# Values that sequencers read, packed in words of 24 bits, in a graph kernel with four residual layers

## The chip, the cores and the metric

The kernel runs on one core of one Trainium2 chip. The metric is the device time of one execution in microseconds (us).

## What is computed

A graph has 3125 nodes with 64 features and 100000 edges, sorted by destination. Four blocks follow each other, each of them `x = x + layer(relu(layernorm(x)))`:

- block 0, three transformer convolutions: for each edge `alpha = q[dst] . (k[src] + e) / 8` with `e = edge_attr_64 @ We`; a softmax of alpha over the edges with the same destination; the sum over these edges of `softmax * (v[src] + e)`; plus `x @ Ws + bs`, relu, and a layer norm after the first two;
- block 1, ten steps of a propagation over the graph, `h = 0.9 * norm * sum(h[src] * norm[src]) + 0.1 * h0`;
- block 2, one graph convolution with degree norms and `edge_attr_32`;
- block 3, one attention layer with a softmax over the edges of a destination.

The three convolutions of block 0 go over the edges; blocks 1 and 3 work with a dense matrix of edge counts that is built on the way.

## The kernel before, in words

Destinations are cut in `NB` = 25 blocks of 128 nodes. Edges come in groups of 128; two groups are a batch (`BT` = 2). There are `NG` = 391 batches of edges, and `T` = `NBAT` = 415 batches of slots, as a batch that crosses into the next block of destinations is gone through once for each block. Which batch of edges, and which block, belongs to slot batch `j` depends on the data: the first phase computes it on VectorE (L456 to L476) and leaves it as rows of int32 on one partition each. SP copies them to where they stay (L306 to L308). The rows are: `ring_row`, the place in the ring of edge batches (0 to 54); `done_row`, how many edge batches must have landed; `brow`, the block (0 to 24); `free_row`, the last slot batch that needs an edge batch (SP frees its place behind it); `w4row`, the column offset in the matrix of edge counts for each of `T4` = 595 window slots; `flag_row`, 0 or 128 for each of these, which picks the zero half or the identity half of `identz`.

`row_values` (L91) emits one TENSOR_LOAD that puts n words of such a row into n registers of one engine's sequencer. In the trace all these loads stand under L93. With `REGS` = 5 the rows that go by `j` are read five words at a time; `w4row` and `flag_row` 17 at a time (`ADJ_ROW`), 3 or 10 at the start of a layer.

The body of `conv(l)` runs once for each layer. All engines work through a list that is written out in full, with semaphores between them.

- POOL (L217) gathers the node rows of each batch of edges with two indirect DMAs, into a ring of `RBAT` = 55 batches, after a wait on `free`.
- SP (L635 to L644) waits until the last user of a ring place is done (`bmm` against a value of `free_row`, L639, L640), gives it free, starts the load of the edge attributes (L642), and reports the batch of four before as landed (L631).
- ACT makes one-hot matrices of the destinations (L678, L681), sums products (L691), copies windows of edge counts out of PSUM (L699) and stores them to memory (`store_counts`, L704 to L710), at an offset from `w4row`.
- PE expands node values to edges (`expand`, L771, with `block_of`), aggregates edges to nodes (`aggregate`, L775 to L789, with `ring_row`), counts sources (L798), and adds window counts (`window_counts`, L812 and L814, with `flag_row`).
- DVE multiplies (`product`, L898 to L908, with `ring_row` and `done_row`), makes the one-hot operands (L916, L917, L924, L926), the weighted one-hots (`weighted`, L939, in layer 2 also L943 with `ring_row`), adds results to their block (`add`, L952, with `block_of`), and does the softmax of a window of up to 90 groups (L959 and on).

Slot batches are cut in windows of 45 batches (eight of them), 30, 15 and 10. While window w goes through expand and product, window w - 1 goes through weighted, aggregate and add. So one step of the loop has batch `j` of the first kind and batch `j` - 45 of the second. Between two windows stands the softmax of the window that was just gone through. Buffers between engines are two or three deep: expand of `j` waits for product `j` - 2, aggregate for add `j` - 2, product for the sums `j` - 3.

```python
if j % REGS == 0:
    regs[1] = row_values(nc, ET.DVE, ring_row, j, REGS, RBAT - 1)
    regs[2] = row_values(nc, ET.DVE, done_row, j, REGS, NG, 1)
dve.wait_ge(s["landed"], regs[2][j % REGS] & 1023)
```

Of the kernel before, what the change touches and what calls it, by code (L numbers as in the profile page):

```python
# [24 lines left out]
ADJ_ROW = 17  # L25
# [14 lines left out]
REGS = 5  # L40
# [87 lines left out]
def build(nc, a, out):  # L128
# [9 lines left out]
    with ctx:  # L138
# [46 lines left out]
        flag_row, done_row, free_row = [arena[32 * q:32 * q + 1, w4:w4 + T4].bitcast(i32) for q in (1, 2, 3)]  # L185
# [69 lines left out]
        with phase(nc, "qp ldd ldx ldw lds cst cio cnt gi ms p1 p2 p3 c1 c2 c3 mm mc st var std h row tr key ktr kc xs wr") as (block, s):  # L255
# [27 lines left out]
            CI, BI, RI, LI, FI, FQ = [V(tmp.take(n), n, dt=i32, parts=1) for n in (T, T, T, T, T4, NG)]  # L283
            SRT = V(tmp.take(NC), NC, dt=i32)
            MQ = V(tmp.take(L * AB), L, AB)
# [4 lines left out]
            def _(sp):  # L290
# [16 lines left out]
                for to, fr in ((ring_row, RI), (brow, BI), (flag_row, FI), (done_row[:, 0:T], LI), (free_row[:, 0:NG], FQ)):  # L307
                    sp.dma_start(to, fr).then_inc(s["wr"], 16)  # L308
# [5 lines left out]
                sp.wait_ge(s["wr"], 16 * 9)  # L314
# [89 lines left out]
            def _(dve):  # L404
                st = Steps(dve, s["st"])
                dve.wait_ge(s["ldd"], 32)
# [55 lines left out]
                st.link(dve.tensor_scalar(BI, WH[:, 0:T], float(NB - 1), None, ALU.min))  # L462
# [10 lines left out]
                st.link(dve.tensor_scalar(RI, CI, float(-(-65536 // RBAT)), None, ALU.mult))  # L473
                st.link(dve.tensor_single_scalar(RI, RI, 16, ALU.logical_shift_right))
                st.link(dve.scalar_tensor_tensor(RI, RI, float(-RBAT), CI, ALU.mult, ALU.add))
# [62 lines left out]
        def conv(l):  # L538
# [67 lines left out]
            with phase(nc, names) as (block, s):  # L606
# [19 lines left out]
                def _(sp):  # L626
# [6 lines left out]
                    last_slots = {}  # L633
# [21 lines left out]
                def _(act):  # L655
# [45 lines left out]
                    def store_counts(k):  # L701

                        t = adj0 + k
                        if k == 0 or t % ADJ_ROW == 0:  # L704
                            wins[0] = row_values(nc, ET.Activation, w4row, t, ADJ_ROW - t % ADJ_ROW, (NW4 - 1) * NB * WIN)
                            wins[1] = t
# [3 lines left out]
                        act.dma_start(adj_t[:, bass.ds(wins[0][t - wins[1]], NB * WIN)], ACC[t % 3]).then_inc(s["kst"], 16)  # L710
# [37 lines left out]
                def _(pe):  # L748
# [26 lines left out]
                    def aggregate(j):  # L775

                        if j % REGS == 0:
                            rings[0] = row_values(nc, ET.PE, ring_row, j, REGS, RBAT - 1)
# [3 lines left out]
                        r = rings[0][j % REGS]  # L782
# [942 lines left out]
```

## Time and profile before

| | us |
|---|---|
| median of 3 runs | 5708.73 |
| the runs | 5693.49, 5708.73, 5719.92 |
| the profiled execution | 5753.34 |
| its span, first to last instruction | 5751.5 |

| engine | busy, us | share of the span |
|---|---|---|
| PE | 3721.8 | 65% |
| DVE | 3245.0 | 56% |
| ACT | 2445.1 | 43% |
| POOL | 2353.9 | 41% |

The mean granted clock of TensorE is 0.76 of its full speed. Register, semaphore and DMA-issuing instructions are run by an engine's sequencer; they are not counted as busy, and the rows give their durations with a q behind the engine's name (DVEq). "Idle before" is the time that the engine stood still just before an instruction; "issue" as its releaser means that it waited for nothing that the profile can name, such as its own sequencer.

### The profile page before, as it was taken

To read this page: it belongs to the slowest core of one execution; us is meant where nothing else is said; L and a number is where in the kernel's file an instruction comes from. 1 tells how busy PE (TensorE), PEld (TensorE's weight loads), DVE (VectorE), ACT (ScalarE), POOL (GpSimd) and SP (SyncE) were. 2 spreads that over 40 slices of the span, in tenths; PEclk is the share of its full clock that TensorE was granted. 3 is DMA by queue.
4 is the path that set the end of the run, shared out by engine and by line. 5 is a ranking of instruction groups with operands and counts; after the bars stand their busy time and mean duration, and the time that the engine had idled before them with its cause. 6 is when DMAs were issued, how large, how long until landed. Compare 5 with 4: busy or idle time off the path is not lost. (4 is left out here: it accounts for less than half of the span.)

```text
span 5751.5 us, 96272 instructions
## 1 busy us (share of the span) xinstructions
PE 3721.8 (65%) x23392; PEld 3092.1 (54%) x23392; DVE 3245.0 (56%) x10295; ACT 2445.1 (43%) x8519; POOL 2353.9 (41%) x2436
## 2 busy tenths in 40 slices
PE   2466666665516666666664277777777749999566
PEld 1355544554414555444443166766666649999322
DVE  5366665565605665665554156656666643334699
ACT  0455555564306555655541265555553320000266
POOL 7255555555071555555532445555555020000000
PEclk9977687777756777777875577767776759999688
DMA  2233333333031333333321223333333040000000
GB/s 67 60 80 82 82 90 95 96 98 83 26 72 52 80 79 80 97 98 96 95 68 40 54 74 81 82 76 78 80 79 74 23 161 2 2 2 2 1 3 4
DMA packets 552348, 372.37 MB, mean 65 GB/s; under 512 B 399844, under 2 KB 476740, under 8 KB 551811
## 3 DMA queue, kind: packets, MB, share of 16 engines
q1 hardware_dynamic: 353891, 144.09, 9.8%
q10 hardware_dynamic: 121536, 142.57, 8.1%
q0 software_dynamic: 76384, 79.48, 7.3%
q8 instruction: 224, 3.67, 0.3%
q14 instruction: 313, 2.56, 0.1%
HBM read 300.59 MB, written 65.24 MB: 64 GB/s over the span
## 5 line engine op out<-in xcount | busy, mean ns | idle before, releaser
L217 POOL DMA_INDIRECT arena<-node_table,arena x1564 | 1513.6, 968 | 1262.6 <-SPq L640 831.8
L784 PE MATMUL ps<-arena 128*128 x4980 | 1078.6, 354 | 374.4 <-issue 150.4
L784 PEld LDWEIGHTS ps<-arena 128*128 128x128 f32 x4980 | 900.8, 254 | 496.0 <-issue 491.7
L908 DVE TENSOR_TENSOR arena<-ps,arena 128x258 f32<-128x258 f32 x1245 | 524.1, 421 | 1056.9 <-issue 706.7
L691 ACT ACTIVATE arena<-arena 128x129 f32<-128x129 f32 x2490 | 743.2, 301 | 794.7 <-DVE arena L908 403.9
L939 DVE TENSOR_SCALAR arena<-arena 128x128 f32<-128x128 uint16 x2490 | 877.9, 357 | 304.6 <-remote 110.8
L217 POOL DMA_INDIRECT arena<-last_node_table,arena x782 | 747.2, 955 | 640.3 <-SPq L640 415.5
L771 PE MATMUL ps<-arena 128*128 x2496 | 557.8, 362 | 193.6 <-issue 134.5
L771 PE MATMUL ps<-arena,e 128*128 x2484 | 551.7, 360 | 143.7 <-issue 69.8
L771 PEld LDWEIGHTS ps<-arena 128*128 128x128 f32 x2496 | 473.3, 257 | 272.6 <-issue 259.1
L1226 PE MATMUL ps<-arena 128*128 128x192 bf16 x6875 | 590.3, 247 | 18.4 <-issue 7.8
L1226 PEld LDWEIGHTS ps<-arena 128*128 128x128 bf16 x6875 | 586.6, 98 | 21.7 <-issue 13.8
L771 PEld LDWEIGHTS ps<-arena,e 128*128 128x128 f32 x2484 | 465.9, 255 | 219.4 <-issue 207.8
L812 PE MATMUL ps<-stage,al 128*128 128x400 bf16 x1190 | 398.2, 427 | 277.6 <-issue 172.1
L691 ACT ACTIVATION_READ_ACCUMULATOR arena<-arena 128x1 f32 x2490 | 468.0, 188 | 0.0
L952 DVE TENSOR_TENSOR arena<-arena,ps 128x129 f32 (+1 forms) x1245 | 363.5, 292 | 156.8 <-issue 59.3
L699 ACT ACTIVATE al<-ps 128x400 bf16<-128x400 f32 x397 | 197.3, 497 | 411.1 <-PE ps L814 113.9
L678 ACT ACTIVATE arena<-arena 128x256 f32<-128x256 bf16 x624 | 312.0, 500 | 93.3 <-issue 63.2
L678 ACT ACTIVATE e<-arena 128x256 f32<-128x256 bf16 x621 | 310.4, 500 | 89.9 <-issue 61.2
L926 DVE TENSOR_SCALAR stage<-arena 128x400 bf16<-128x400 uint16 x1190 | 345.0, 331 | 0.0
L789 PEld LDWEIGHTS ps<-arena 128*128 128x128 f32 x1660 | 309.4, 261 | 0.0
L789 PE MATMUL ps<-arena 128*128 x1660 | 293.7, 309 | 0.0
(340 smaller groups left out, 4209.4 us busy)
## 6 DMA issues: line engine op xcount, KB each, us to landing
arena<-in_attr SPq DMA_DIRECT2D x1173, 96.0 KB
arena<-slot_rows ACTq DMA_DIRECT2D x249, 320.0 KB
edge_counts<-al ACTq DMA_DIRECT2D x397, 100.0 KB
arena<-node_table,arena POOLq DMA_INDIRECT x1564
edge_counts<-stage ACTq DMA_DIRECT2D x198, 100.0 KB
arena<-last_node_table,arena POOLq DMA_INDIRECT x782
arena<-edge_counts SPq DMA_DIRECT2D x24, 500.0 KB, 5.4
stage<-edge_counts SPq DMA_DIRECT2D x16, 500.0 KB, 5.8
```

Source lines behind the costliest of these rows:

```text
L217: pool.indirect_dma_start(out=RING[:, t % R_SLOTS, XO:XO + n], out_offset=None, in_=table[:, :], in_offset=bass.IndirectOffsetOnAxis(ap=ID ...
L678: act.activation(o, ROWB[r % 2][:, (j % 5) * BT * P:(j % 5 + 1) * BT * P], ACT.Square, bias=pid1, scale=-1.0)\
L691: ins = act.activation(PR[j % 3][:, q], PR[j % 3][:, q], ACT.Copy, accum_out=AL[w % 2][:, c:c + 1])
L771: ins = pe.matmul(UPS[j % 2][:, q * AB:(q + 1) * AB], OHT[j % 6][:, q * P:(q + 1) * P], U[:, bass.ds(b, 1), :].rearrange("p a b -> p (a b) ...
L784: ins = pe.matmul(BPS[j % 2][:, 0:AB], WOH[j % 2][:, q], RINGS[:, bass.ds(r, 1), q, D32:D32 + AB].rearrange("p o f -> p (o f)"), start=q = ...
L789: ins = pe.matmul(BPS[j % 2][:, AB:CW], WOD[j % 2][:, q], RINGS[:, bass.ds(r, 1), q, 0:D32].rearrange("p o f -> p (o f)"), start=q == 0, s ...
L812: ins = pe.matmul(WPS, LOH[k % 3][:, q], KOH[k % 3][q], start=q == 0, stop=t == 0 and q == G4 - 1)
L908: dve.tensor_tensor(PR[j % 3], UPS[j % 2].rearrange("p (a b) -> p a b", b=AB), rows, ALU.mult)\
L926: ins = dve.tensor_scalar(KOH[k % 3][q], iota1[:, 0:NB * WIN], KEY4[:, adj0 + k, q:q + 1], None, ALU.is_equal)
L939: ins = dve.tensor_scalar(WOH[j % 2][:, q], iota1[:, 0:P], DZT[:, t:t + 1], PT[w % 2][:, c:c + 1], ALU.is_equal, ALU.mult)
L952: dve.tensor_tensor(to, to, BPS[j % 2], ALU.add).then_inc(s["add"], 1)
L1226: last = pe.matmul(ps[:, o + 256 * c:o + 256 * c + 3 * D], adj3[:, sx, bass.ds((d0 + c) * P, P)], g3[:, sx].rearrange("p a b -> p (a b)"), ...
```

## The change

The rows for sequencers are packed on VectorE in the first phase, several values in a word of at most 24 bits, and read a word at a time. `row_values` goes; `word_value` reads one word, `word_values` n words, and `field` takes a value out of a word by shift and mask.

- `REGS` is 4. `brow` has 4 blocks of 5 bits in a word. `ring_row` has two words for four batches: 4 ring places of 6 bits, and then the landed count of the first batch with the differences of the other three (2 bits each). `done_row` goes.
- `w4row` has 3 windows of 8 bits in a word (`ADJ_WIN` = 3), and the offset is multiplied out on ACT's sequencer. `flag_row` has 17 flags of one bit in a word.
- `free_row` is not packed; SP reads its words one at a time.

```diff
-def row_values(nc, eng, row, at, n, top, low=0):
+def word_value(nc, eng, row, at):
+
+    return word_values(nc, eng, row, at, 1)[0]
+
+
+def word_values(nc, eng, row, at, n):
 
     return nc.values_load_multi_w_load_instructions(
-        row[0:1, at:at + n], engines=[eng], min_val=low, max_val=top,
-        skip_runtime_bounds_check_because="the rows hold groups, blocks and windows of slots, which are in range for any edges")[1]
+        row[0:1, at:at + n], engines=[eng], min_val=0, max_val=(1 << 24) - 1,
+        skip_runtime_bounds_check_because="the words hold fields of 24 bits together")[1]
+
+
+def field(nc, word, at, bits, top):
+
+    v = (word >> at) & ((1 << bits) - 1) if at else word & ((1 << bits) - 1)
+    return nc.s_assert_within(v, 0, top, skip_runtime_bounds_check_because="the fields hold groups, blocks and windows of slots, in range for any edges")
...
+                def pack(to, values, per, bits):
+
+                    n = values.shape[1]
+                    full, words = n // per, -(-n // per)
+                    part = PK[:, 0:words]
+                    if words > full:
+                        st.link(dve.memset(part, 0.0))
+                    for k in range(per):
+                        v = values[:, k::per]
+                        if k:
+                            st.link(dve.scalar_tensor_tensor(part[:, 0:v.shape[1]], v, float(1 << bits * k), part[:, 0:v.shape[1]],
+                                                             ALU.mult, ALU.add))
+                        else:
+                            st.link(dve.tensor_copy(part[:, 0:v.shape[1]], v))
+                    st.link(dve.tensor_copy(to[:, 0:words], part))
...
-                st.link(dve.tensor_scalar(BI, WH[:, 0:T], float(NB - 1), None, ALU.min))
+                st.link(dve.tensor_scalar(WH[:, 0:T], WH[:, 0:T], float(NB - 1), None, ALU.min))
+                pack(BI, WH[:, 0:T], REGS, 5)
...
-                st.link(dve.tensor_scalar(w4row, WH[:, 0:T4], float(NB * WIN), None, ALU.mult))
+                pack(w4row, WH[:, 0:T4], ADJ_WIN, 8)
...
-                st.link(dve.tensor_scalar(FI, FR[:, 0:T4], float(P), None, ALU.mult))
+                pack(FI, FR[:, 0:T4], ADJ_ROW, 1)
...
-                dve.tensor_scalar(LI, CI, 1.0, None, ALU.add)
...
+                pack(RI[:, 0::2], WH[:, 0:T], REGS, 6)
+                st.link(dve.tensor_scalar(WH[:, 0:NREG], CI[:, 0::REGS], 1.0, None, ALU.add))
+                for k in range(1, REGS):
+                    n = CI[:, k::REGS].shape[1]
+                    st.link(dve.tensor_tensor(PK[:, 0:n], CI[:, k::REGS], CI[:, 0::REGS][:, 0:n], ALU.subtract))
+                    st.link(dve.scalar_tensor_tensor(WH[:, 0:n], PK[:, 0:n], float(1 << 7 + 2 * k), WH[:, 0:n], ALU.mult, ALU.add))
+                st.link(dve.tensor_copy(RI[:, 1:2 * NREG:2], WH[:, 0:NREG]))
...
-                            at = i - RBAT + 1
-                            if at % REGS == 1:
-                                last_slots[0] = row_values(nc, ET.SP, free_row, at, min(REGS, NG - RBAT + 1 - at), T, 1)
-                            sp.wait_ge(s["bmm"], last_slots[0][(at - 1) % REGS] & 1023)
+                            sp.wait_ge(s["bmm"], word_value(nc, ET.SP, free_row, i - RBAT + 1) & 1023)
...
-                        if k == 0 or t % ADJ_ROW == 0:
-                            wins[0] = row_values(nc, ET.Activation, w4row, t, ADJ_ROW - t % ADJ_ROW, (NW4 - 1) * NB * WIN)
-                            wins[1] = t
+                        if k == 0 or t % ADJ_WIN == 0:
+                            wins[0] = word_value(nc, ET.Activation, w4row, t // ADJ_WIN)
...
-                        act.dma_start(adj_t[:, bass.ds(wins[0][t - wins[1]], NB * WIN)], ACC[t % 3]).then_inc(s["kst"], 16)
+                        act.dma_start(adj_t[:, bass.ds(field(nc, wins[0], 8 * (t % ADJ_WIN), 8, NW4 - 1) * (NB * WIN), NB * WIN)], ACC[t % 3]).then_inc(s["kst"], 16)
...
                         if j % REGS == 0:
-                            rings[0] = row_values(nc, ET.PE, ring_row, j, REGS, RBAT - 1)
+                            rings[0] = word_value(nc, ET.PE, ring_row, j // REGS * 2)
...
-                        r = rings[0][j % REGS]
+                        r = field(nc, rings[0], 6 * (j % REGS), 6, RBAT - 1)
...
-                            flags[0] = row_values(nc, ET.PE, flag_row, t, ADJ_ROW - t % ADJ_ROW, P)
-                            flags[1] = t
+                            flags[0] = word_value(nc, ET.PE, flag_row, t // ADJ_ROW)
...
-                            ins = pe.matmul(WPS, identz[:, bass.ds(flags[0][t - flags[1]], P)], ACC[(t - 1) % 3], start=False, stop=True)
+                            ins = pe.matmul(WPS, identz[:, bass.ds(field(nc, flags[0], t % ADJ_ROW, 1, 1) * P, P)], ACC[(t - 1) % 3], start=False, stop=True)
...
                         if j % REGS == 0:
-                            regs[0] = row_values(nc, ET.PE, brow, j, REGS, NB - 1)
-                        return regs[0][j % REGS]
+                            regs[0] = word_value(nc, ET.PE, brow, j // REGS)
+                        return field(nc, regs[0], 5 * (j % REGS), 5, NB - 1)
...
                         if j % REGS == 0:
-                            regs[1] = row_values(nc, ET.DVE, ring_row, j, REGS, RBAT - 1)
-                            regs[2] = row_values(nc, ET.DVE, done_row, j, REGS, NG, 1)
-                        dve.wait_ge(s["landed"], regs[2][j % REGS] & 1023)
+                            regs[1], regs[2] = word_values(nc, ET.DVE, ring_row, j // REGS * 2, 2)
+                        k, done = j % REGS, regs[2] & 511
+                        dve.wait_ge(s["landed"], done + ((regs[2] >> (7 + 2 * k)) & 3) if k else done)
```

DVE's `block_of` and the ring place in `weighted` (layer 2 alone) change in the same way as PE's. `RI` has `2 * NREG` words (`NREG` = 104), the copies of SP take only the packed words, and one of them, that of `done_row`, goes.

## Rows read from the trace of the kernel before

**Rows 1.** Busy time by stage; the loops are the second, third and fourth.
```profile
core 0: us, PE busy (x) PEld busy (x) DVE busy (x) ACT busy (x) POOL busy (x), PEclk, DMA share, GB/s
0.00:218.00 218.00, 44.52 (x196) 36.68 (x197) 85.76 (x202) 11.57 (x22) 144.23 (x153) 1.00 0.29 68
218.00:1528.00 1310.00, 847.42 (x4522) 668.98 (x4521) 792.77 (x2914) 737.12 (x2753) 648.01 (x672) 0.77 0.32 82
...
1726.00:3054.00 1328.00, 839.57 (x4516) 662.60 (x4517) 792.94 (x2914) 736.86 (x2752) 650.83 (x672) 0.76 0.32 81
...
3253.00:4597.00 1344.00, 984.13 (x5317) 879.05 (x5317) 808.63 (x2911) 673.89 (x2611) 644.28 (x673) 0.71 0.29 70
4597.00:5751.00 1154.00, 901.26 (x8422) 752.64 (x8422) 666.47 (x1082) 256.68 (x317) 44.76 (x27) 0.85 0.07 22
```

**Rows 2.** Line 93, all loads of registers: ns min/median/max, first and last start.
```profile
L93 DVEq TENSOR_LOAD <-arena x860: 583/1302/1666, 214.1 to 4620.7; - x172
L93 PEldq TENSOR_LOAD <-arena x535: 587/1407/4365, 215.5 to 4616.5; - x179
L93 SPq TENSOR_LOAD <-arena x204: 17/1064/1375, 214.3 to 4466.8; - x102
L93 ACTq TENSOR_LOAD <-arena x37: 711/3657/3840, 229.9 to 4317.7; - x37
```

**Rows 3.** Line 93, single loads: ACT with 3, 10, 17, 17 words, SP with 5, 1.
```profile
L93 ACTq TENSOR_LOAD <-arena x1: 711/711/711, 3277.4 to 3277.4; - x1
...
L93 ACTq TENSOR_LOAD <-arena x1: 2175/2175/2175, 1750.5 to 1750.5; - x1
...
L93 ACTq TENSOR_LOAD <-arena x1: 3652/3652/3652, 2631.6 to 2631.6; - x1
...
L93 ACTq TENSOR_LOAD <-arena x1: 1247/1247/1247, 2571.0 to 2571.0; - x1
...
L93 SPq TENSOR_LOAD <-arena x1: 1069/1069/1069, 2497.9 to 2497.9; - x1
...
L93 SPq TENSOR_LOAD <-arena x1: 268/268/268, 4466.8 to 4466.8; - x1
```

**Rows 4.** Line 93, DVE's loads of 5 words in a group of layer 1.
```profile
L93 DVEq TENSOR_LOAD <-arena x2: 807/1102/1398, 2488.0 to 2488.9; - x2
...
L93 DVEq TENSOR_LOAD <-arena x1: 1257/1257/1257, 2493.0 to 2493.0; - x1
```

**Rows 5.** Line 908, the product, in windows 1 to 7 of layers 0, 1, 2.
```profile
L908 DVE TENSOR_TENSOR arena<-ps,arena x315: 407/422/429, 308.7 to 1299.3; 128x258 f32<-128x258 f32 x158
...
L908 DVE TENSOR_TENSOR arena<-ps,arena x315: 408/422/429, 1834.0 to 2821.1; 128x258 f32<-128x258 f32 x158
...
L908 DVE TENSOR_TENSOR arena<-ps,arena x315: 406/420/429, 3354.6 to 4342.5; 128x258 f32<-128x258 f32 x158
```

**Rows 6.** Timeline of DVE around these loads: start, us, instruction, idle before.
```profile
2489.30 0.34 DVE L939 TENSOR_SCALAR arena<-arena 128x128 f32<-128x128 uint16 x1
2490.59 0.42 DVE L908 TENSOR_TENSOR arena<-ps,arena 128x258 f32<-128x258 f32 x1 [0.95 <-issue]
...
2492.93 0.35 DVE L939 TENSOR_SCALAR arena<-arena 128x128 f32<-128x128 uint16 x1
2494.44 0.29 DVE L952 TENSOR_TENSOR arena<-arena,ps 128x129 f32 x1 [1.17 <-issue]
```

**Rows 7.** Lines 903 and 908, register instructions ahead of the product at 2490.59.
```profile
L903 DVEq ALU_OP  x1: 40/40/40, 2490.3 to 2490.3; - x1
...
L908 DVEq FUSED_REGOPS  x1: 69/69/69, 2490.5 to 2490.5; - x1
```

**Rows 8.** Waits of SP's queue: us in total, times, longest.
```profile
SPq L640 <- PE ps L784: 1181.3, 291, 101.5
```

**Rows 9.** Timeline at the end of the first phase, DVE.
```profile
122.69 2.75 DVE L881 MEMSET arena<- 128x3225 f32 x1 [35.34 <-PEq L88]
```

**Rows 10.** Line 217, POOL's gathers, with what ended POOL's idle time before them.
```profile
L217 POOL DMA_INDIRECT arena<-node_table,arena x1564: 938/944/1917, 48.8 to 2953.0; - x196
L217 POOL DMA_INDIRECT arena<-last_node_table,arena x782: 938/944/1210, 3117.2 to 4473.5; - x196
its engine sat idle before it (us, times) until:
  SPq L640: 1247.3, 451
  issue: 590.6, 1892
```

More of the change, by code:

```diff
@@ L24 @@
 ADJ_AT = [sum(ADJ_N[:k]) for k in range(3)]
-ADJ_ROW = 17
+ADJ_ROW, ADJ_WIN = 17, 3
+NWW, NFL = -(-T4 // ADJ_WIN), -(-T4 // ADJ_ROW)
 NBAT = sum(WIN_BATCHES)
@@ L39 @@
 EARLY, LOADS, LAG = 24, 8, 4
-REGS = 5
+REGS = 4
+NREG = -(-T // REGS)
 HIST = NC // 4
@@ L184, in build @@
         w4row = V(w4, T4, dt=i32, parts=1)
-        flag_row, done_row, free_row = [arena[32 * q:32 * q + 1, w4:w4 + T4].bitcast(i32) for q in (1, 2, 3)]
+        flag_row, free_row = [arena[32 * q:32 * q + 1, w4:w4 + T4].bitcast(i32) for q in (1, 2)]
         iota0 = V(mem.take(P // 2), P, dt=u16)
@@ L282, in build @@
             TR = V(tmp.take(IW), IW, parts=1)
-            CI, BI, RI, LI, FI, FQ = [V(tmp.take(n), n, dt=i32, parts=1) for n in (T, T, T, T, T4, NG)]
+            CI, BI, QI, RI, FI, FQ = [V(tmp.take(n), n, dt=i32, parts=1) for n in (T, T, T, 2 * NREG, T4, NG)]
             SRT = V(tmp.take(NC), NC, dt=i32)
+            PK = V(tmp.take(NWW * ADJ_WIN), NWW * ADJ_WIN, parts=1)
             MQ = V(tmp.take(L * AB), L, AB)
@@ L306, in _ @@
                 sp.wait_ge(s["c1"], 1)
-                for to, fr in ((ring_row, RI), (brow, BI), (flag_row, FI), (done_row[:, 0:T], LI), (free_row[:, 0:NG], FQ)):
+                for to, fr in ((ring_row[:, 0:2 * NREG], RI[:, 0:2 * NREG]), (brow[:, 0:NREG], BI[:, 0:NREG]), (flag_row[:, 0:NFL], FI[:, 0:NFL]),
+                               (free_row[:, 0:NG], FQ)):
                     sp.dma_start(to, fr).then_inc(s["wr"], 16)
@@ L313, in _ @@
                 sp.wait_ge(s["ldw"], 16 * 9)
-                sp.wait_ge(s["wr"], 16 * 9)
+                sp.wait_ge(s["wr"], 16 * 8)
             @block.gpsimd
@@ L466, in _ @@
                 st.link(dve.tensor_scalar(WH[:, 0:T4], WH[:, 0:T4], float(NW4 - 1), None, ALU.min))
-                st.link(dve.tensor_scalar(w4row, WH[:, 0:T4], float(NB * WIN), None, ALU.mult))
+                pack(w4row, WH[:, 0:T4], ADJ_WIN, 8)
                 st.link(dve.memset(FR[:, 0:1], 1.0))
                 st.link(dve.tensor_tensor(FR[:, 1:T4], WH[:, 1:T4], WH[:, 0:T4 - 1], ALU.not_equal))
-                st.link(dve.tensor_scalar(FI, FR[:, 0:T4], float(P), None, ALU.mult))
+                pack(FI, FR[:, 0:T4], ADJ_ROW, 1)
                 dve.tensor_scalar(FQ, FS[0:1, :], 1.0 / BT, None, ALU.mult)
-                dve.tensor_scalar(LI, CI, 1.0, None, ALU.add)
-                st.link(dve.tensor_scalar(RI, CI, float(-(-65536 // RBAT)), None, ALU.mult))
-                st.link(dve.tensor_single_scalar(RI, RI, 16, ALU.logical_shift_right))
-                st.link(dve.scalar_tensor_tensor(RI, RI, float(-RBAT), CI, ALU.mult, ALU.add))
+                st.link(dve.tensor_scalar(QI, CI, float(-(-65536 // RBAT)), None, ALU.mult))
+                st.link(dve.tensor_single_scalar(QI, QI, 16, ALU.logical_shift_right))
+                st.link(dve.scalar_tensor_tensor(WH[:, 0:T], QI, float(-RBAT), CI, ALU.mult, ALU.add))
+                pack(RI[:, 0::2], WH[:, 0:T], REGS, 6)
[5 more added lines that the diff above has]
+                st.link(dve.tensor_copy(RI[:, 1:2 * NREG:2], WH[:, 0:NREG]))
                 dve.sem_inc(s["c1"], 1)
@@ L631, in report @@
                         sp.sem_inc(s["landed"], 1)
-                    last_slots = {}
                     for i in range(NG):
                         if i >= RBAT:
-                            at = i - RBAT + 1
-                            if at % REGS == 1:
-                                last_slots[0] = row_values(nc, ET.SP, free_row, at, min(REGS, NG - RBAT + 1 - at), T, 1)
-                            sp.wait_ge(s["bmm"], last_slots[0][(at - 1) % REGS] & 1023)
+                            sp.wait_ge(s["bmm"], word_value(nc, ET.SP, free_row, i - RBAT + 1) & 1023)
                             sp.sem_inc(s["free"], 1)
@@ L906, in product @@
                             dve.wait_ge(s["ra"], j - 2)
-                        rows = RINGS[:, bass.ds(regs[1][j % REGS], 1), :, D32:D32 + AB].rearrange("p o q f -> p (o q) f")
+                        rows = RINGS[:, bass.ds(field(nc, regs[1], 6 * (j % REGS), 6, RBAT - 1), 1), :, D32:D32 + AB].rearrange("p o q f -> p (o q) f")
                         dve.tensor_tensor(PR[j % 3], UPS[j % 2].rearrange("p (a b) -> p a b", b=AB), rows, ALU.mult)\
@@ L932, in weighted @@
                         if last and q == 0 and j % REGS == 0:
-                            regs[3] = row_values(nc, ET.DVE, ring_row, j, REGS, RBAT - 1)
+                            regs[3] = word_value(nc, ET.DVE, ring_row, j // REGS * 2)
                         if q == 0:
@@ L941, in weighted @@
                         if last:
-                            scale = RINGS[:, bass.ds(regs[3][j % REGS], 1), q, RW - 1:RW].rearrange("p o f -> p (o f)")
+                            scale = RINGS[:, bass.ds(field(nc, regs[3], 6 * (j % REGS), 6, RBAT - 1), 1), q, RW - 1:RW].rearrange("p o f -> p (o f)")
                             ins = dve.tensor_scalar(WOD[j % 2][:, q], iota1[:, 0:P], DZT[:, t:t + 1], scale, ALU.is_equal, ALU.mult)
@@ L991, in block_of @@
                         if j % REGS == 0 or 0 not in regs:
-                            regs[0] = row_values(nc, ET.DVE, brow, j, REGS, NB - 1)
-                        return regs[0][j % REGS]
+                            regs[0] = word_value(nc, ET.DVE, brow, j // REGS)
+                        return field(nc, regs[0], 5 * (j % REGS), 5, NB - 1)
                     def first(w):
```

## The prediction

> **What bounds the kernel.** I read the stages first. The three edge loops hold 3982 of 5751 us, and in none of them is an engine full: in layer 0, 1310 us, PE is busy 847, DVE 793, ACT 737, POOL 648 [rows 1]. So the loops are limited by waits between engines and by sequencers. Next I took the rows of the instructions that the diff touches: the loads of registers. DVE runs 860, PE 535, SP 204, ACT 37 of them; DVE's have a median of 1.30 us, ACT's 3.66 [rows 2]. Their sequencer does nothing else meanwhile; the engine lives on what was already queued.
>
> How is a load priced? By the word. ACT's load of 3 words takes 0.711, of 10 words 2.175, of 17 words 3.652: (2.175 - 0.711) / 7 = 0.209 a word, and some 0.08 fixed. SP's loads of 5 words take 1.069 and of 1 word 0.268: 0.200 a word [rows 3]. One exception: every fourth of ACT's 17-word loads takes 1.247 [rows 3]; the start moves on by 17 words each time, so these are the ones that start at the same place modulo four, and 1.247 is 5 reads where 3.652 is 17 (four words in one read, and a last one). DVE's first load in the group shown took 0.807 for its 5 words (2 reads), the second 1.398 (5 reads), so 0.197 a read there too [rows 4]. DVE and PE have no shorter load. One word on DVE: at most 0.807 - 0.197 = 0.61; two words at most 0.81. DVE's fastest 5-word load, 0.583, gives 0.39 and 0.58 as the low side [rows 2]. I take 0.5 and 0.7.
>
> Does a load show? From the 315 starts of the product (L908) in windows 1 to 7 of each layer, first and last in [rows 5], I took the distance of each start from the one before. Where j is a multiple of 5, which is where DVE loads ring places and landed counts, it is on average 4.29, 3.95 and 5.03 us in layers 0, 1, 2; elsewhere 2.61, 2.68 and 2.43. The excess is 1.69, 1.27 and 2.61 us per five batches. In layer 2 DVE loads the ring row once more at the batches of the second kind, which are multiples of 5 at the same steps. The timeline shows one case: DVE's loads run from 2488.0 to 2490.3 [rows 4], its queue is empty at 2489.64, and the product starts at 2490.59 after 0.95 us idle. The block load of 1.257 us at 2493.0 [rows 4] leaves 1.17 us idle before the add at 2494.44 [rows 6]. Within the multiples of 5, groups with one quick load were 0.41 us shorter at 0.47 us less load time: the exposed part follows the load almost one for one.
>
> **The change, part by part.** The sum is made against the profiled execution (5753.3 us, 0.8% above the median of 5708.7).
> 1. *Pair before the product.* Two loads of 5 words (about 2.4 us, quick and full-length ones weighed together) every 5 batches become one of 2 words (0.7) every 4. About 2.4 - 1.4 = 1.0 us was covered by the queue, more than 0.7, so the excess goes: 83 groups x (1.69 + 1.27 + 2.61) = 462 us. I leave 0.1 us showing at each of 312 new pairs: -430. Bounds: 462, and 215 if PE's ring load at the same batches, which shrinks too but less, or the lockstep keeps half.
> 2. *Block loads*, DVE and PE, 1.2 to 1.4 us to 0.5: some show as in [rows 6], mostly hidden: -30 (0 to -80).
> 3. *17-word loads* of ACT and PE. 37 each; those of full length, up to 3.84 and 4.37 us [rows 2], 28 of each. Summing the distances of starts over the eight steps around one of full length in windows 1 to 7, against the mean of their residues, gives +2.4 us (PE, 14 cases) and +1.9 us (ACT, 15). 28 x 4.3 = 120. PE then loads one word 37 times, and ACT one word some 200 times at 0.27 us (less in all than its 37 long ones): -90 (-40 to -130).
 Most runs ahead under a filled queue; what stands between a wait and its instruction shows. I take one sixth, by the share of such instructions that lay in DVE's gaps over these windows (35 us in some 990, at seven a batch): 600 / 6 = +100. Bounds 0 and +600.
> 5. *SP.* Its 201 loads of 5 words become 1005 of one word (the three that already had one stay): 1008 x 0.27 = 270 us of SP instead of 182. They stand ahead of the wait on bmm, in which SP sits anyway, 1181 us on L784 alone [rows 8]; behind SP's wait stand free, POOL's gathers, the attribute load and the report of landings. Cost 0; without that cover 0.1 us a batch.
> 6. *Setup.* Packing adds about 40 linked DVE operations on one partition, at about 0.2 us by the neighbours of that stage: +8 us, under the 35.34 us in which DVE waits for the barrier [rows 9]. One fewer row is copied. 0.
> 7. *What is late next.* A batch needs two gathers of 0.94 us with 0.30 between them, 2.5 us; 391 batches are 977 us of a loop of 1310, and POOL mostly waits for freed slots, 1247 us in all [rows 10]. With a loop near 1190 it has less slack, but is not the bound. Landings and PE's own waits will take back part: +90, an estimate (0 to +200).
>
> Sum: -430 - 30 - 90 + 100 + 90 = -360, so 5393 in a profiled execution, and 5349 from the median; as the given-back part rests on nothing measured, I round towards no change: **5365 us**.
>
> [...]
>
> **Rivals.**
> A. *Another wait takes the place.* For: in DVE's gaps in these windows more time is plain waiting for others than loads. PE's loads, ACT's copies or a landing would end the step instead. Then only a third of terms 1 to 3 stays: 550 / 3 - 80 for fields = 100 less, 5600. Against: the slope above.
> B. *A load on DVE or PE costs the same whatever its words* (their rows all have 5 or more). Pair 2.4 to 1.2: 0.2 shows 312 times, 62 instead of 31 us; block loads are as dear but more frequent, PE has 661 instead of 535, and ACT's 200 cost 1.2 us each, so that its share of term 3 goes. Of the 360 us, 31 go for pairs, 30 for blocks, 80 for ACT and 30 for PE: a gain of about 190, 5520. Against: quick and slow loads on DVE differ by the reads. Chance small.
> C. *Slower: the fields stand in series on the lockstep path.* Place: behind the waits of expand, aggregate, product and add, once each per batch. Price: 0.49 us a batch, 610 us, against 462 + 80 + 130 = 672 at best, 255 at the low bounds. It decides from 0.2 us a batch shown (255 / 1245); with 0.3 shown (370 us) and the loads at their low bounds the time is 5709 + 370 - 255 = 5825. For: the trace shows the register instruction right before the product [rows 7]. Against: only a sixth of them now lies in gaps.
> D. *Nothing to see*: the steps are held by matmuls and the ring, and what the loads free is waited away. For: POOL's long wait for freed slots [rows 10]. Against: the steps differ by where the loads stand [rows 5]. 5709.
>
> **Chances.** Forecast 0.64, A 0.16, B 0.06, C 0.08, D 0.06. Faster by over 0.5% (what a measurement can tell here): the first three, less a little, 0.85; same 0.07; slower 0.08. The range takes in the forecast's bounds (terms 1 to 3 in full and few fields: 5709 - 540 = 5170) and rival A: up to 5620.
>
> **What would show it.** DVE's loads near 740 with a median of 0.5 to 0.7 us, PE's near 660, SP's 1008 at 0.27, ACT's near 200 at 0.29. The distance of products where j is a multiple of 4 falls to about 2.7, the others stay near 2.5. Loops of about 1190 to 1210 us each, the time between and after them unchanged. DVE's issue idle before L908 falls by more than half; register instructions rise by about 3000 on DVE and on PE. Wrong if the loads of one or two words still take 1.2 us (B), if DVE's idle time moves to waits for PE or landings (A), or if steps away from the loads grow by over 0.2 us (C).

## The result, and the profile after

The changed kernel took 5624.4 us (median, 5619.7 to 5634.7) against 5712.0 us for the kernel before on the same chip: ratio 0.985, 95% interval 0.983 to 0.988. The gain is 88 us where 344 were forecast, and the time lies 4 us above the range. The profiled execution has a span of 5620.5 us.

The loads of registers came out as forecast. The answer to [rows 2]:

```profile
L100 SPq TENSOR_LOAD <-arena x1008: 7/266/1137, 216.9 to 4357.1; - x168
L100 DVEq TENSOR_LOAD <-arena x734: 6/530/989, 216.2 to 4496.8; - x184
L100 PEldq TENSOR_LOAD <-arena x661: 5/473/738, 217.5 to 4492.9; - x166
L100 ACTq TENSOR_LOAD <-arena x201: 275/281/477, 228.3 to 4466.2; - x101
```

DVE's loads took 1032 us in all before (the sum of their durations) and take 408 now, PE's 758 and 299. The three edge loops, to be read against the second to fourth stage of [rows 1]:

```profile
219.00:1478.00 1259.00, 850.34 (x4523) 642.67 (x4522) 804.46 (x2914) 742.57 (x2754) 647.78 (x672) 0.79 0.34 86
1670.00:2945.00 1275.00, 852.76 (x4516) 650.81 (x4517) 804.07 (x2914) 739.94 (x2752) 653.59 (x676) 0.78 0.34 85
3134.00:4473.00 1339.00, 978.26 (x5326) 864.55 (x5326) 851.21 (x2911) 681.21 (x2615) 646.54 (x680) 0.72 0.30 71
```

The loops fell by 51, 53 and 5 us; 1190 to 1210 us each had been expected. The peak at the loads is gone: in layer 0 the product's mean distances for j = 0, 1, 2, 3 modulo 4 are 2.98, 2.73, 2.75, 2.99 us (the first step of each window left out), where the multiples of 5 had 4.29. But the steps away from the loads grew, from 2.59, 2.64 and 2.45 us in the three layers to 2.82, 2.90 and 3.06. The mean of all steps went from 2.90, 2.88 and 2.92 us to 2.86, 2.87 and 3.00: the time was moved from one step to the others. Over windows 1 to 7 the product (L941, against [rows 5]) needs nearly as long as before:

```profile
L941 DVE TENSOR_TENSOR arena<-ps,arena x315: 409/426/430, 301.3 to 1260.3; 128x258 f32<-128x258 f32 x158
L941 DVE TENSOR_TENSOR arena<-ps,arena x315: 408/426/430, 1771.2 to 2728.2; 128x258 f32<-128x258 f32 x158
L941 DVE TENSOR_TENSOR arena<-ps,arena x315: 409/427/430, 3235.7 to 4228.8; 128x258 f32<-128x258 f32 x158
```

That is 959, 957 and 993 us, against 991, 987 and 988. The product's own line says where its time went (the count, then ns min/median/max; under it what its engine's idle time waited for, us and times; "remote" is a semaphore for which the profile names no sender):

```profile
L941 DVEq ALU_OP  x2178: 2/45/1387, 219.7 to 4471.4; - x198
...
  issue: 342.0, 317
  remote: 319.8, 109
  PE ps L805: 140.2, 92
```

The same list for L908 in the kernel before began:

```profile
  issue: 706.7, 370
  PE ps L771: 157.8, 78
  remote: 103.8, 25
```

So the "issue" time fell by more than half, as forecast, but "remote" time took the place of much of it.

Two more things stand out. Besides its fused instruction, each product had no register instruction before; now there are 2178 for 1245 products, not one each, and line 936, the landed count, has 3111 where L903 had one per product. And single ones took up to 1.39 us where the median is 0.045. In all the trace has 14,438 instructions more than that of before (110,710 against 96,272).

### The profile page after: what moved, and what is told of

It is laid out like the page before. It is cut to its first block and busy times, and to the rows that moved or that the text cites. A ratio compares the mean times of both kernels' runs of the same rounds, so it can differ in the third digit from the quotient of the medians.

```text
span 5620.5 us, 110710 instructions
## 1 busy us (share of the span) xinstructions
PE 3733.9 (66%) x23392; PEld 3043.0 (54%) x23392; DVE 3320.8 (59%) x10335; ACT 2459.9 (44%) x8519; POOL 2351.6 (42%) x2436
## 5 line engine op out<-in xcount | busy, mean ns | idle before, releaser
L230 POOL DMA_INDIRECT arena<-node_table,arena x1564 | 1514.9, 969 | 1180.2 <-SPq L675 761.2
L818 PE MATMUL ps<-arena 128*128 x4980 | 1080.9, 352 | 418.7 <-issue 175.9
L818 PEld LDWEIGHTS ps<-arena 128*128 128x128 f32 x4980 | 880.3, 248 | 559.5 <-issue 553.5
L941 DVE TENSOR_TENSOR arena<-ps,arena 128x258 f32<-128x258 f32 x1245 | 528.6, 425 | 905.9 <-issue 342.0
L230 POOL DMA_INDIRECT arena<-last_node_table,arena x782 | 743.7, 951 | 645.1 <-SPq L675 428.6
L972 DVE TENSOR_SCALAR arena<-arena 128x128 f32<-128x128 uint16 x2490 | 873.8, 355 | 217.5 <-PE ps L818 89.2
L805 PE MATMUL ps<-arena 128*128 x2496 | 558.4, 361 | 170.2 <-issue 77.8
L805 PEld LDWEIGHTS ps<-arena 128*128 128x128 f32 x2496 | 454.3, 252 | 267.0 <-issue 262.6
L805 PEld LDWEIGHTS ps<-arena,e 128*128 128x128 f32 x2484 | 445.4, 247 | 205.9 <-issue 201.9
L845 PE MATMUL ps<-stage,al 128*128 128x400 bf16 x1190 | 380.3, 410 | 183.7 <-issue 115.5
L976 DVE TENSOR_SCALAR arena<-arena 128x128 f32<-128x128 uint16 x830 | 297.5, 358 | 19.3 <-issue 15.1
L823 PEld LDWEIGHTS ps<-arena 128*128 128x128 f32 x1660 | 303.8, 257 | 0.3 <-issue 0.3
```

What stands on the lines that cost most here:

```text
L230: pool.indirect_dma_start(out=RING[:, t % R_SLOTS, XO:XO + n], out_offset=None, in_=table[:, :], in_offset=bass.IndirectOffsetOnAxis(ap=ID ...
L805: ins = pe.matmul(UPS[j % 2][:, q * AB:(q + 1) * AB], OHT[j % 6][:, q * P:(q + 1) * P], U[:, bass.ds(b, 1), :].rearrange("p a b -> p (a b) ...
L818: ins = pe.matmul(BPS[j % 2][:, 0:AB], WOH[j % 2][:, q], RINGS[:, bass.ds(r, 1), q, D32:D32 + AB].rearrange("p o f -> p (o f)"), start=q = ...
L823: ins = pe.matmul(BPS[j % 2][:, AB:CW], WOD[j % 2][:, q], RINGS[:, bass.ds(r, 1), q, 0:D32].rearrange("p o f -> p (o f)"), start=q == 0, s ...
L845: ins = pe.matmul(WPS, LOH[k % 3][:, q], KOH[k % 3][q], start=q == 0, stop=t == 0 and q == G4 - 1)
L941: dve.tensor_tensor(PR[j % 3], UPS[j % 2].rearrange("p (a b) -> p a b", b=AB), rows, ALU.mult)\
```

## The experiments

**Two kinds of chip.** The unedited kernel before came out at two times: 4823 to 4828 us in four sets of runs, on three chips, and 5762 us in one set, on a fourth; the times above, 5712 us, are of the second kind as well. "Kind" is only a name for the two times: whether it belongs to the chip or to its condition at the hour, no run shows. Every ratio below is against before on the same chip, and "first kind" means 4825 us, "second kind" 5700 to 5760.

**1. Fields with the long loads.** The kernel before, but ring places, blocks and landed counts are stored shifted up and taken out again on PE and DVE, here PE's ring place:

```diff
-r = rings[0][j % REGS]
+r = field(nc, rings[0][j % REGS], 6, 6, RBAT - 1)
```

> The kernel before, with its five-word and 17-word loads, but every ring place, block and landed count is stored shifted up and taken out again by a shift and a mask (about as many register instructions on VectorE and TensorE as in the changed kernel: some 8,400 and 5,000). Theory P (the fields stand behind a wait on the path and cost what the loads gave): 5950 to 6060 us. Theory R (any recorded instruction on any engine costs, some 25 per us being the most that the core issues): the same, 5950 to 6060. Theory L (the fields are cheap as predicted, the shorter loads were simply worth little): 5720 to 5800.

First kind: 1.048 (1.045 to 1.052), 5065 us: 238 us for 12,096 more register instructions. The times expected above are for the second kind; as ratios to 5709 us, theories P and R gave 1.042 to 1.061, and L, by which the fields are cheap, at most 1.016. L falls here.

**2. Four words, no fields.** Each row starts at a multiple of four words, one value per word; ring places and landed counts stand side by side:

```diff
-ADJ_ROW = 17
+ADJ_ROW = 4
...
-REGS = 5
+REGS = 4
...
-    regs[1] = row_values(nc, ET.DVE, ring_row, j, REGS, RBAT - 1)
-    regs[2] = row_values(nc, ET.DVE, done_row, j, REGS, NG, 1)
+    words = row_values(nc, ET.DVE, ring_row, 2 * j, 2 * REGS, 1023)
+    regs[1], regs[2] = [place(nc, v) for v in words[0:4]], words[4:8]
```

(`place` only tells the compiler the range of a value.)

> Short loads without fields: one value per word, rows that start at a multiple of four words, four values per load (ring places and landed counts of four batches side by side in one load of eight), four words for flags and windows. Register instructions as in the kernel before. Theories P and R: 5300 to 5420 us, the gain that was predicted with no price for fields. Theory L: 5580 to 5640, like the changed kernel.

First kind: 0.935 (0.932 to 0.938), 4515 us, in the range of P and R as a ratio.

**3. Fields ahead of the waits.** The changed kernel with shift and mask written to a register before the wait:

```diff
+r = early(pe, rings[0], 6 * (j % REGS), 6, RBAT - 1)
 pe.wait_ge(s["woh"], j + 1)
...
-r = field(nc, rings[0], 6 * (j % REGS), 6, RBAT - 1)
```

> The changed kernel with the same loads and the same number of register instructions, but ring places and blocks on VectorE and TensorE are shifted and masked into a register ahead of the waits of their instruction, so that they run while the engine waits. Theory P: 5420 to 5520 us. Theories R and L: 5600 to 5640, no change.

First kind: 0.950 (0.947 to 0.953), 4595 us. The changed kernel itself gave 0.954 on this kind (run 6), 4597 us. The place of the fields is worth little or nothing, so theory P falls: they cost something, but not because they stand behind a wait.

**4. Register instructions on GpSimd.**

```diff
+for k in range(18):
+    pool.reg_alu(idle, idle, 1, ALU.logical_shift_left)
+    pool.reg_alu(idle, idle, 1, ALU.logical_shift_right)
 gather(pool, i, table, XG)
```

> The changed kernel with six more register instructions (36 shifts, fused) on GpSimd for each batch's gather, some 6,900 in all, about half as many as the change added; GpSimd has idle time in each step. Theory R: 5720 to 5800 us. Theories P and L: 5610 to 5650.

First kind: 0.954 (0.951 to 0.957), 4612 us. The changed kernel without these instructions has the same ratio (run 6). The 6876 instructions are in the trace at 149 ns each, and cost nothing that can be measured. On this kind of chip theory R falls.

**5 and 6. Both kernels, unedited, on one chip.**

> The kernel before, unedited, for its trace on the chip of these runs. In the first four runs it took 4828 us where the traces on record ran 5751 us with 169 instructions stretched to about 0.7 us each. Theory B (the recorded chip held every engine back in stretches, one instruction per 0.7 us, and more instructions meant more of it): ratio 1.00; where the time is near 4830 us fewer than 20 such stretched instructions, where it is near 5700 us over 100.

> The changed kernel, unedited. Theory B: if the kernel before takes about 4830 us here, ratio 0.950 to 0.957 (the run with more work on GpSimd gave 0.954) and hardly any stretched instruction; if it takes about 5700 us, 0.983 to 0.988 and over 500 of them. Theory F (the fields alone ate the gain, on any chip): 0.98 to 0.99 in both cases.

First kind: 1.000 and 0.954 (0.952 to 0.955), 4825 and 4597 us. Register instructions that took over 0.2 us, those on POOL left out: none in either, where the traces of the second kind have 144 and 809. The loops of the changed kernel there (columns as in [rows 1]), and its product:

```profile
155.00:1179.00 1024.00, 754.92 (x4519) 564.07 (x4519) 794.80 (x2914) 727.78 (x2752) 686.42 (x710) 0.88 0.43 109
1269.00:2310.00 1041.00, 759.82 (x4524) 564.08 (x4522) 799.60 (x2914) 730.16 (x2752) 735.60 (x758) 0.88 0.44 111
2401.00:3436.00 1035.00, 810.33 (x5323) 707.73 (x5323) 834.34 (x2912) 676.44 (x2611) 723.62 (x758) 0.86 0.42 98
...
L941 DVEq ALU_OP  x2178: 40/45/45, 155.0 to 3435.4; - x198
...
  SPq L670: 185.0, 177
  issue: 129.7, 210
```

The same 2178 instructions never took over 45 ns. PE is busy 755 us in layer 0 instead of 850, at a granted clock of 0.88 of full speed instead of 0.79 (means over stretches, each at half or at full speed in the trace). The first cause named for the product's idle time is now SP's report of landed gathers (L670); in the kernel before, on the same chip, "issue" was first with 259.5 us and that report had 133.7. And POOL (L230, against [rows 10]) hardly ever waits for a freed slot:

```profile
L230 POOL DMA_INDIRECT arena<-node_table,arena x1564: 938/944/2155, 48.4 to 2249.3; - x196
L230 POOL DMA_INDIRECT arena<-last_node_table,arena x782: 940/944/1191, 2371.0 to 3354.4; - x196
its engine sat idle before it (us, times) until:
  issue: 663.7, 2177
  SPq L675: 128.2, 166
```

In layer 2 the gathers run from 2371.0 to 3354.4, 983 us for 391 batches, 2.51 us each. Before, on the same chip, that idle line read:

```profile
  issue: 645.0, 2116
  SPq L640: 269.4, 227
```

**7 and 8. Fields on one engine.** Run 2 with a redundant shift and mask, on DVE alone and on PE alone (the other engine has rows of its own):

```diff
+v = (word >> at) & ((1 << bits) - 1) if fields else word
```

> The short loads of four words of the second run, with a redundant shift and mask on each ring place, block and landed count on VectorE alone (some 7,100 more register instructions). That run and the changed kernel differ by 0.954 - 0.935 = 1.9%, for the fields on both engines. If VectorE sets the step: 0.948 to 0.955 here. If TensorE does: 0.935 to 0.940.

> The same with the redundant shift and mask on TensorE alone (some 5,000 more register instructions), VectorE without. If TensorE sets the step: 0.948 to 0.955. If VectorE does: 0.935 to 0.940. If both stand in one chain, in each of the two about half of the 1.9%.

0.944 (0.942 to 0.945) and 0.940 (0.939 to 0.942), on the chip of runs 5 and 6. Against 0.935 that is some 42 us for DVE's 7067 more register instructions and 27 us for PE's 4980: neither engine alone sets the step. Both prices are a little low, as PE's loads from rows of its own took 338 ns in the median, 504 in run 2.

**9 to 12. On a chip of the second kind.** Run 2 with a memset on POOL ahead of each batch's two gathers; run 2 and the kernel before with only one of the two gathers once the ring is full, which leaves half of the rows in the ring stale; and before with only the pair of loads ahead of the product changed as in run 2.

```diff
+st.link(pool.memset(SPARE, 0.0))
 gather(pool, i, table, XG)
```
```diff
-for t in range(BT * i, BT * i + BT):
+for t in range(BT * i, BT * i + (BT if i < RBAT else 1)):
...
-sp.wait_ge(got[i % RBAT], 16 * BT * (l * len(range(i % RBAT, NG, RBAT)) + i // RBAT + 1))
+sp.wait_ge(got[i % RBAT], 16 * (l * (len(range(i % RBAT, NG, RBAT)) + 1) + i // RBAT + 2))
```

> The short loads of four words (0.935), with one 128x128 memset more on GpSimd ahead of each batch's two gathers. GpSimd issued a batch's gathers every 2.50 us all through the loops of that run (391 x 2.50 = 978 us a layer, of loops of 998 to 1022). Theory G (the gathers' issue is what bounds the loops once the loads are short): 0.2 to 0.3 us x 1149 batches = 230 to 350 us more, ratio 0.98 to 1.01. Not G: 0.935 to 0.945, as six register instructions per batch there cost nothing measurable (0.954 in both).

> The short loads of four words, with only one of the two gathers of each batch from the 56th batch of a layer on; half the rows of node values there are stale, so the output is not the reference's. Theory G: the loops fall under 978 us to what TensorE and VectorE need, ratio 0.88 to 0.91. Not G: 0.925 to 0.935.

> The kernel before with its long loads, and the same half of the gathers left out. Theory G: before was held by gathers only in part (GpSimd waited 269 us for free places), so 0.97 to 0.99; and the distance to the run with short loads and half the gathers opens from 313 us to 400 to 480 us, what the prediction priced for the loads. Not G: 0.99 to 1.00, distance 313 us as before.

> The kernel before, with the pair of loads ahead of a product (ring places and landed counts, five words each) alone replaced by one load of eight aligned words per four batches; all other loads long. If the terms of the prediction hold in their proportion (430 of 550 us), three quarters of the 6.5%: 0.948 to 0.955. If the pair's excess was partly that of other loads of the same step: 0.960 to 0.975. If only the pair counts and then the gathers bound: 0.935 to 0.945.

Measured: 0.968 (0.966 to 0.970), 0.790 (0.789 to 0.792), 0.885 (0.884 to 0.887) and 0.991 (0.989 to 0.994); in us 5575, 4556, 5097, 5714, before 5762. None of the four lies in a range that was expected: those were made for the first kind. Run 9 doesn't answer for that kind, for which it was meant; the half of the gathers was worth far more here than either theory had it. The pair alone, 430 of the predicted 550 us, brought 48 us. Its product in windows 1 to 7 of layer 0, and that of runs 9, 10 and 11:

```profile
L923 DVE TENSOR_TENSOR arena<-ps,arena x315: 409/421/429, 306.6 to 1292.7; 128x258 f32<-128x258 f32 x158
```
```profile
L924 DVE TENSOR_TENSOR arena<-ps,arena x315: 409/420/429, 295.3 to 1257.9; 128x258 f32<-128x258 f32 x158
```
```profile
L922 DVE TENSOR_TENSOR arena<-ps,arena x315: 406/418/430, 299.1 to 983.3; 128x258 f32<-128x258 f32 x158
```
```profile
L908 DVE TENSOR_TENSOR arena<-ps,arena x315: 409/419/429, 307.8 to 1096.6; 128x258 f32<-128x258 f32 x158
```

With all gathers it is 986 us (run 12) and 963 us (run 9), whatever the loads are. With half of them it is 684 us (run 10) and 789 us (run 11).

**13 to 16. The same questions on the first kind.**

> Short loads of four words without fields, as in the second run. Theory G (gathers bound the loops as soon as the rest is faster, at 2.50 us a batch on the chips where before takes 4825 us, at about 2.85 us on those where it takes 5700 to 5760): ratio 0.930 to 0.940 on the first kind, 0.970 to 0.985 on the second, where the run with one load changed gave 0.991 and the one with a memset 0.968. Theory F (the fields were what ate the gain of the changed kernel): 0.93 to 0.94 on both kinds.

> The changed kernel beside it on the same chip. Theory G: 0.950 to 0.957 on the first kind, 0.980 to 0.990 on the second, within 1% of the run with four words. Theory F: over 4% slower than the run with four words on the second kind.

> Long loads and half the gathers from the 56th batch of a layer on (stale rows of node values, so the output is not the reference's). On a chip of the second kind again 0.885. On one of the first kind, theory G: 0.97 to 0.99, near 4730 us; there before waits for gathers little.

> Four words and half the gathers (stale rows too). On a chip of the second kind again 0.790. On the first kind, theory G: 0.86 to 0.90, so that the distance to the run above is 400 to 550 us, as the 541 us between them on the second kind; with the gathers whole it was 313 us there. Not G: distance 313 us.

Measured: 0.933 (0.931 to 0.936), 0.953 (0.950 to 0.956), 0.995 (0.992 to 0.997) and 0.885 (0.882 to 0.888); 4504, 4601, 4803, 4270 us, before 4824. So on this kind the half of the gathers costs the kernel with long loads almost nothing (21 us), and the one with short loads 234 us. The product in windows 1 to 7 of layer 0, runs 15 and 16:

```profile
L908 DVE TENSOR_TENSOR arena<-ps,arena x315: 408/419/429, 243.0 to 1037.6; 128x258 f32<-128x258 f32 x158
```
```profile
L922 DVE TENSOR_TENSOR arena<-ps,arena x315: 406/416/430, 234.7 to 919.0; 128x258 f32<-128x258 f32 x158
```

795 and 684 us: with half the gathers the two kinds of chip agree (789 and 684 in runs 11 and 10).

**17 and 18. Fields without the gathers' cover, and four words once more.**

> The changed kernel with half the gathers from the 56th batch of a layer on (stale rows of node values, so the output is not the reference's). With long loads 4803 us and with four words 4270 us were measured so where before takes 4824 us, 5097 and 4556 us where it takes 5762. Fields in proportion to the 96 us of the whole gathers: 4350 to 4400 us on the first kind of chip, 4640 to 4690 on the second (ratio 0.905 to 0.915 and 0.805 to 0.815). If the fields were partly hidden by the gathers: over 4400 and over 4700 us.

> Short loads of four words, all gathers. On a chip of the first kind again 0.930 to 0.940. On one of the second kind theory G: 0.970 to 0.985, as the gathers' pace there stands over the loops however short the loads are. Theory F (there the fields ate the gain): 0.93 to 0.94.

First kind again: 0.922 (0.920 to 0.925), 4450 us, and 0.934 (0.932 to 0.936), 4508 us. With half the gathers the fields cost 180 us (4450 - 4270), over the 80 to 130 that were expected, and with all of them 96; so part of them lies under the gathers. Run 2's kernel on the second kind of chip was not measured without the memset; run 9 is the nearest to it.

## Why the prediction was wrong

The runs put a number to most of the terms; terms 5 and 6, put at nothing, were not tested by themselves. With half the gathers, on the first kind of chip, they are taken from 4803 (long loads), 4270 (four words) and 4450 us (changed kernel). I take half the gathers to stand for a kernel in which the gathers take nothing back. Term 7 is then the difference between this column and the others:

| term | predicted, us | half the gathers | all, first kind | all, second kind |
|---|---|---|---|---|
| 1 to 3, shorter loads | -550 | -533 | -320 | not run |
| 4, fields | +100 | +180 | +96 | not run |
| 7, what is late next | +90 | (0) | +130 | +265 |
| the change in all | -360 | -353 | -223 | -88 |

Against the forecast of -360 the second kind is off by 272 us: 17 from the loads, 80 from the fields, 175 from term 7.

**Terms 1 to 3, the loads: right in sum.** Four words aligned to four cost nearly what one does. From run 13, whose loads are of four words, and on DVE of four and eight:

```profile
L94 DVEq TENSOR_LOAD <-arena x734: 344/568/1153, 151.1 to 3383.7; - x184
L94 ACTq TENSOR_LOAD <-arena x151: 304/308/712, 162.6 to 3332.0; - x151
```

ACT's took 0.308 us for four words against 0.281 for one, DVE's 0.568 against 0.530, and with eight words about 0.81. So the price by reads holds, and rival B with its flat price falls. The column "half the gathers" takes the four-word kernel as the short loads without fields, not quite the loads of the change. How the 533 us divide among the three terms no run shows.

**Term 4, the fields: the share was right, the count was not.** I wrote that a shift and a mask cost about one more instruction, 6019 in all. That rested on four steps to an instruction, which no trace shows; run 4 has six in one. A field of the lowest place costs one instruction, each other two, as neither is fused with the address (312 + 2 x 933 = 2178 for 1245 products). The landed count takes 2.5 on average. DVE and PE have 12,464 more ALU_OP, twice what was counted. 180 us / 12,464 = 14 ns of some 0.08 us from start to start (in run 6, median 74 ns on DVE and 97 on PE): about a sixth shows, as I had taken, and 20 ns in run 1. Rival C had them stand in series behind the waits; moving them ahead of the waits (run 3) brought at most 0.4%, inside the intervals. Its sign, steps away from the loads that grow by over 0.2 us, did come: by 0.2, 0.3 and 0.6 us. But the sign doesn't tell the fields from the gathers: run 9, which has no fields, has a mean step of 2.89 us in layer 0 on this kind of chip, the changed kernel 2.86.

**Term 7, what is late next: this is the step that failed.** "With a loop near 1190 it has less slack, but is not the bound", and +90 us with an upper bound of 200. What was given back is the difference of the columns: 353 - 223 = 130 us on the first kind, inside the bound, and 353 - 88 = 265 us on the second, outside it. The 353 is carried over from the first kind, as the changed kernel was not run with half the gathers on the second; the loads alone gave 541 us there and 533 on the first, so it should carry. On the first kind the whole change gave 4.6% where the forecast was 6.0%.

The prediction's own price fits the first kind: two gathers a batch take 2.5 us, 978 us a layer, against loops of 1023 to 1040 us in which POOL hardly waits for slots. On the second kind windows 1 to 7 take 957 to 993 us in all three layers of both kernels, and 963 to 986 in layer 0 of runs 9 and 12. For some 297 of the 391 batches of edges (315 x 391 / 415) that is 3.2 to 3.3 us a batch. POOL's issuing is not what bounds there: its gathers take the same 944 ns, and in the changed kernel it still waits for freed slots, nearly as long as in [rows 10]:

```profile
  SPq L675: 1189.8, 504
  issue: 568.9, 1839
```

It is the other engines that run slower while all gathers are made, and with half of them they don't (684 and 789 us in runs 10 and 11, against 684 and 795 on the first kind). So with all gathers there is a floor of 3.2 to 3.3 us a batch, whatever the loads. The kernel before already stood at it, which fits the little that shorter loads gained, and no idle cause names it: the product's line says "issue" and "remote".

The other side of it shows where no gathers run. In windows 9 and 10, when all batches are in, the product of before spans, in layer 0 on the second kind and on the first:

```profile
L908 DVE TENSOR_TENSOR arena<-ps,arena x25: 409/421/428, 1445.0 to 1527.3; 128x258 f32<-128x258 f32 x25
```
```profile
L908 DVE TENSOR_TENSOR arena<-ps,arena x25: 411/420/427, 1157.1 to 1239.4; 128x258 f32<-128x258 f32 x25
```

82.3 us on both. The changed kernel, on the second kind:

```profile
L941 DVE TENSOR_TENSOR arena<-ps,arena x25: 415/426/429, 1403.6 to 1477.1; 128x258 f32<-128x258 f32 x25
```

73.5 us: 10.7% less, on a chip where the whole kernel gained 1.5%. Of the 931 us between the two profiled executions of before (5751.5 and 4820.5), 63 lie ahead of the first product, 657 in the loops and 211 in the two stretches between them, where the ring is filled (199 and 200 us against 93 and 95 us). Behind the loops, where there are no gathers, both take 1155 us.

Could the second kind be slower by TensorE's clock alone? The loop of layer 0 of before on the first kind (run 5), to be read against the second stage of [rows 1]:

```profile
155.00:1240.00 1085.00, 738.54 (x4520) 586.74 (x4519) 783.34 (x2914) 726.42 (x2752) 691.44 (x709) 0.85 0.40 102
```

On the second kind the granted clock is lower, 0.77 against 0.85, and PE is busy for 109 us more (847 against 739). The loop is 225 us longer, so the clock can be about half of it at most. In windows 9 and 10 the clock is 0.87 on both.

**Rival A** (another wait takes the place, 5600 us, 0.16) was the nearest in time and in kind. I had looked for it in PE's loads, ACT's copies or a landing; with all gathers and short loads it was the gathers. Its "for" was right there in the trace: most of DVE's gaps were waiting for others. Taking +90 for term 7, "an estimate" on nothing measured, with 200 as its bound, was the choice that put the range wrong.

**What stays open.** Why the gathers slow everything on chips of the second kind and not on the three of the first. The stretched register instructions go with it but don't explain it: run 9 has the fewest of the runs with all gathers there (67 over 0.2 us, where the changed kernel has 809) and is at the same 960 us. A limit on recorded instructions per us, my first theory for that chip (the 25 of theory R, an estimate of mine), falls too: in windows 1 to 3 of layer 0 before has 19 to 20 a us, the changed kernel 24 and run 10 31. A memset between one batch's gathers and the next's shortened the stretches between the loops from about 200 us (192 and 200 in run 10, which has the same loads) to 134 and 122 us (run 9). So there, gathers that follow each other without a pause are part of it; inside the loops, 963 us in windows 1 to 7 are no better than the 957 to 993 of kernels without a memset. No run separates the making of the transfers from their traffic.

**A version that beats both**: four aligned words per load and no fields, 0.933 to 0.935 in three sets of runs on two chips of the first kind, against 0.953 to 0.954 for the changed kernel. Its product waits mostly for landings (run 13), as it should where the gathers are the bound:

```profile
  SPq L644: 276.3, 249
  issue: 95.0, 142
  PE ps L785: 55.5, 54
```

On the second kind it was measured only with the memset, 0.968 against 0.985.

## What to carry to other kernels

Price what a sequencer reads by aligned groups of four words before packing fields: here four values in a load cost nearly what one does (0.308 against 0.281 us on ACT), and every shift and mask was an instruction of its own. When the pace of an engine (here 2.5 us of gathers a batch) times its count comes within a fifth of the loop that you forecast (978 of 1190 us), don't put a small number for what it gives back: halve that work in the kernel before and in the cheapest form of the change, and measure. Two such runs showed here what no row of idle causes did. The pace alone would not have done: on the second kind of chip it gives 978 us, and the loops took 1259 to 1339. Where absolute times differ between chips, compare stretches in which the suspected resource is idle.

## What was not expected of the hardware

- The same program took 4825 us on three chips and 5712 to 5762 us in two other sets of runs. All of the difference lay in the part with gathers; windows without gathers took 82.3 us on both, and what stands behind the loops 1155 us on both.
- GpSimd computes registers under its gathers: 6876 instructions of 149 ns, 1.02 ms in all, cost nothing that shows (run 4).
- The 36 shifts on one register in run 4 came out as six instructions on GpSimd (6876 under one line for 1149 batches, 149 ns each), so more steps fit in one than the four named in the description of the kernel before; the shift and mask of a field stayed two all the same.
